# Attention and mixture-of-experts kernel: 64 value columns as the stationary operand of the attention product, w_v2 applied afterwards

## The reference

```python
xn = layernorm(x)
q, k = xn @ w_q, xn @ w_k                       # 64 columns each
p = softmax(where(causal, q @ k.T / 8, -inf))   # in each batch, 1024 x 1024
attention = p @ ((xn @ w_v1) @ w_v2)            # w_v1 128 x 64, w_v2 64 x 128
logits = xn @ w_router.T                        # 16
s = sigmoid(logits of the best expert e)
y = ((s * xn) @ up[e] * silu((s * xn) @ gate[e])) @ down[e]
shared = (silu(xn @ w_gate.T) * (xn @ w_up.T)) @ w_down.T
out = x + attention + shared + y
```

## Time and profile before

| what | before |
|---|---|
| time of the launch, three runs | 218.82, 219.39, 219.52 us; median 219.39 |
| span of the profiled execution | 222.3 us, which is its own time too (nothing lies around it) |
| PE, DVE, ACT, POOL busy | 207.7, 149.8, 128.7, 146.9 us |

### The profile page before, as it was taken

How to read it: one execution, slowest core, us unless ns; L and a number is a source line. 1 busy time by engine, 2 the same in 40 slices (tenths; PEclk the granted TensorE clock), 3 DMA queues, 4 the chain that set the end, 5 groups by cost and what they waited for, 6 DMA issues and landing times.

```text
span 222.3 us, 4940 instructions
## 1 busy us (share of the span) xinstructions
PE 207.7 (93%) x1405; PEld 180.4 (81%) x1405; DVE 149.8 (67%) x358; ACT 128.7 (58%) x305; POOL 146.9 (66%) x278
## 2 busy tenths in 40 slices
PE   4999999999999999999997999999999989967993
PEld 4787888887777898899895878999997969845893
DVE  2986969879767578868783648766664666425733
ACT  2475977876566756867756356444444436536641
POOL 3465785930388888888831378898989898872200
PEclk9999999999999999999999999999999999999999
DMA  5999999994063118215423222223232321004963
GB/s 156 291 383 306 222 265 175 156 238 201 13 173 103 36 39 200 74 44 141 127 56 79 51 67 73 80 60 90 78 92 63 86 75 41 3 0 156 312 195 97
DMA packets 26951, 28.30 MB, mean 127 GB/s; under 512 B 2579, under 2 KB 23066, under 8 KB 26288
## 3 DMA queue, kind: packets, MB, share of 16 engines
q1 hardware_dynamic: 24400, 23.77, 42.5%
q0 software_dynamic: 2528, 4.24, 6.1%
HBM read 14.28 MB, written 10.50 MB: 111 GB/s over the span
## 4 chain that ended last, share of the span: by engine, by line
PE 66%; issue 11%; POOL 11%; DVE 3%; DMA 3%; ACT 3%; another core or an unknown queue 1%; POOLq 0%; SPq 0%; ACTq 0%; DVEq 0%
PE acc L1368 13%; PE mid L1349 7%; PE acc L1235 6%; PE big L1175 5%; POOL y_rows L515 5%; PE big L1177 4%; PE big L1176 4%; PE acc L1454 4%; PE big L1336 4%; PE big L1333 4%; DMA xe<-scratch 3%; PE big L1368 2%; PE mid L1185 2%; PE mid L1205 2%; PE acc L1196 2%
## 5 line engine op out<-in xcount | busy, mean ns | idle before, releaser
L515 POOL DMA_INDIRECT y_rows<-y,ids x47 | 46.9, 998 | 11.9 <-issue 8.3
L463 POOL DMA_INDIRECT scratch<-rows,slot x32 | 34.2, 1067 | 17.8 <-DVE slot L744 12.7
L1368 PE MATMUL acc<-vr_all,pt 128*128 128x128 f32 x246 | 35.7, 280 | 4.0 <-issue 2.3
L1368 PEld LDWEIGHTS acc<-vr_all,pt 128*128 128x128 f32 x246 | 31.6, 191 | 6.2 <-issue 4.4
L794 DVE TENSOR_REDUCE negmax<-big 128x1 f32<-128x128 f32 (+7 forms) x32 | 23.9, 755 | 14.4 <-PE big L1336 9.5
L1067 ACT COPY pt<-mid 128x512 f32<-128x512 f32 (+3 forms) x48 | 22.8, 476 | 17.8 <-PE mid L1349 14.4
L896 DVE COPY eht<-mid 128x512 f32<-128x512 f32 (+1 forms) x24 | 16.3, 681 | 24.5 <-PE mid L1443 16.4
L1140 ACT COPY y<-acc 128x256 f32<-128x256 f32 (+1 forms) x24 | 8.8, 367 | 36.7 <-PE acc L1454 23.6
L1055 ACT ACTIVATE prob<-big,negmax 128x128 f32<-128x128 f32 (+7 forms) x32 | 23.8, 743 | 10.7 <-DVE negmax L794 7.8
L1454 PEld LDWEIGHTS acc<-wed,eht 128*128 128x128 f32 x188 | 24.3, 191 | 3.3 <-issue 1.7
L1454 PE MATMUL acc<-wed,eht 128*128 x188 | 25.4, 277 | 0.5 <-DVE eht L896 0.4
(11 more groups left out here) (142 smaller groups left out, 465.0 us busy)
## 6 DMA issues: line engine op xcount, KB each, us to landing
we_raw<-w_gate_up SPq DMA_DIRECT2D x4, 1024.0 KB, 10.5
scratch<-blank SPq DMA_DIRECT2D x1, 3120.0 KB, 30.3
xe<-scratch SPq DMA_DIRECT2D x24, 130.0 KB
q_raw<-qk_all SPq DMA_DIRECT2D x8, 256.0 KB
k_raw<-qk_all SPq DMA_DIRECT2D x8, 256.0 KB
wed<-w_down SPq DMA_DIRECT2D x1, 2048.0 KB, 34.4
expert_out<-y_rows SPq DMA_DIRECT2D x8, 256.0 KB, 4.8
out<-res SPq DMA_DIRECT2D x7, 256.0 KB, 3.3
```

The source lines that it names most:

```text
L463: pool.indirect_dma_start(scratch, bass.IndirectOffsetOnAxis(ap=slot[:, t:t + 1], axis=0), rows[:, t, :], None).then_inc(row_sent[t % FLY] ...
L515: pool.indirect_dma_start(y_rows, bass.IndirectOffsetOnAxis(ap=ids[:, t:t + 1], axis=0), y[p % NY][:, t % 2, :], None, bounds_check=NT * P ...
L1368: last = pe.matmul(weighed(b, g, r), pt[n % 2][:, cols], v, start=kb == 0 and (r == 0 or own_bank), stop=True, skip_group_check=True)
```

## The change

- The product of w_v1 and w_v2 at the start goes (two more warm-up transposes stand in its place). `vr_all` holds 64 values and 16 logits for a tile: `project_logits` is 128x80 for each tile, and ACT takes four tiles in one copy. w_v2 gets a tile of its own, `wv2`, and a DMA of its own.
- `weigh(b, n)` is one FP32 product for a block. The 64 value columns of the key tile are stationary, the block in `pt` (up to 512 columns) moves. An even key tile writes to partitions 0 to 63 of `acc`, an odd one to 64 to 127, so in one or the other half of the array's columns.
- The sums of a half are then copied to `mixed` (`keep_mixed`: ACT for g = 0, DVE for g = 1), and `outputs(b, g)` multiplies them by w_v2, which stands there twice, once for the even and once for the odd sums: four 128x128 products for a half. For the last half of batch 3 these are `keep_last` and `last_output`, after all products of the batch. `add_attention` waits for these products (`mixed_out`, `last_out`) in place of those of `weigh`.
- There are four buffers `pt` instead of two, and PE runs the products in groups of four (or two, on the edges of the expert stage); transposes, scores and `outputs` move around them.

```diff
-    VR = P + NE
+    VR = KD + NE
...
-                           + [(f"pt{n}", [P, GC], F32) for n in range(2)])
...
+                           + [(f"pt{n}", [P, GC], F32) for n in range(PTS)]
+                           + [(f"mixed{g}", [P, GC], F32) for g in range(BG)])
...
+            sp.dma_start(wv2[:, :], w_small[:, V20:V20 + P]).then_inc(wv2_loaded, 16)
...
+            def keep_mixed(b, g):
+
+                dve.wait_ge(pv_done, FIRST + b * STEPS + (STEPS if g else GT))
+                dve.tensor_copy(mixed[g][:, :], acc[g][:, :]).then_inc(mixed_kept[g], 1)
...
-                    dve.wait_ge(pv_done, FIRST + b * STEPS + (STEPS if g else GT))
+                    dve.wait_ge(mixed_out[g], b + 1)
...
-                        dve.wait_ge(pv_done, FIRST + b * STEPS + 2 * GT + t + 1)
+                        dve.wait_ge(last_out, t + 1)
...
+                if not first:
+                    keep_mixed(b - 1, 1)
                 if b == B - 1:
+                    row_max(b, BT - 1)
                     add_attention(b - 1, 1)
-                    row_max(b, BT - 1)
                     return
...
-                act.copy(vr_all[:, g * GT:g * GT + GT - 1, :],
-                         mid[0][:, 0:(GT - 1) * VR].rearrange("p (t n) -> p t n", n=VR)).then_inc(vr_kept[u], 1)
-                act.copy(flat(vr_all[:, g * GT + GT - 1:(g + 1) * GT, :]), acc[u][:, 0:VR]).then_inc(vr_kept[u], 1)
+                act.copy(flat(vr_all[:, g * GT:(g + 1) * GT, :]), mid[0][:, 0:GT * VR]).then_inc(vr_kept[u], 1)
...
-                act.copy(pt[n % 2][:, c0:GC], mid[n % 2][:, c0:GC]).then_inc(pt_ready, 1)
+                act.wait_ge(pv_done, FIRST + b * STEPS + n + 1 - PTS if b or n >= PTS else FIRST)
+                act.copy(pt[n % PTS][:, c0:GC], mid[n % 2][:, c0:GC]).then_inc(pt_ready, 1)
...
+            def keep_last(part):
+
+                act.wait_ge(pv_done, FIRST + B * STEPS)
+                cols = slice(part * GC // 2, (part + 1) * GC // 2)
+                act.copy(mixed[1][:, cols], acc[1][:, cols]).then_inc(last_kept, 1)
...
                     keep_pt(b, 0)
+                    keep_pt(b, 1)
                     exp(b, BT - 2)
-                    keep_pt(b, 1)
                     keep_pt(b, 2)
+                    keep_pt(b, 3)
                     exp(b, BT - 1)
-                    keep_pt(b, 3)
+                keep_mixed(b, 0)
                 keep_pt(b, GT)
...
-            pe.matmul(mid[1][:, 0:P], ws_raw[0:KD, V10:V10 + P], ws_raw[0:KD, V20:V20 + P], start=True, stop=True
-                      ).then_inc(v12_done, 1)
...
-                for r in range(c0 // P, GT):
-                    cols = slice(r * P, (r + 1) * P)
-                    own_bank = isinstance(b, int) and b == B - 1 and g == 1
-                    last = pe.matmul(weighed(b, g, r), pt[n % 2][:, cols], v, start=kb == 0 and (r == 0 or own_bank),
-                                     stop=True, skip_group_check=True)
-                last.then_inc(pv_done, 1)
+                half = kb % 2 * KD
+                pe.matmul(acc[g][half:half + KD, c0:GC], flat(vr_all[:, b * BT + kb:b * BT + kb + 1, 0:KD]),
+                          pt[n % PTS][:, c0:GC], start=kb < 2, stop=True, skip_group_check=True
+                          ).then_inc(pv_done, 1)
+
+            def to_output(b, g, r):
+
+                keys = KD if g == 0 and r == 0 else P
+                return pe.matmul(weighed(b, g, r), mixed[g][0:keys, r * P:(r + 1) * P], wv2[0:keys, :], start=True,
+                                 stop=True, skip_group_check=True)
+
+            def outputs(b, g):
+
+                if b == 0 and g == 0:
+                    pe.wait_ge(wv2_loaded, 16)
+                pe.wait_ge(mixed_kept[g], b + 1)
+                for r in range(GT):
+                    last = to_output(b, g, r)
+                last.then_inc(mixed_out[g], 1)
+
+            def last_output(r):
+
+                pe.wait_ge(last_kept, r // 2 + 1)
+                to_output(B - 1, 1, r).then_inc(last_out, 1)
...
+                    transposes(b, 0)
+                    transposes(b, 1)
+                    if b < B - 1:
+                        scores(b, BT - 1)
+                    else:
+                        outputs(b - 1, 1)
+                transposes(b, 2)
+                transposes(b, 3)
+                for n in range(GT):
+                    weigh(b, n)
+                if not first and b < B - 1:
+                    outputs(b - 1, 1)
...
+                transposes(b, GT)
+                transposes(b, GT + 1)
+                outputs(b, 0)
+                transposes(b, GT + 2)
+                transposes(b, GT + 3)
...
+                scores(following, 0)
+                for n in range(GT, 2 * GT):
                     weigh(b, n)
...
+                for n in range(2 * GT, STEPS):
+                    weigh(b, n)
+                scores(following, GT + 1)
+                scores(following, GT + 2)
```

More of the change, by code:

```diff
@@ L1378, in first_half @@
                     pe.wait_ge(ranks_used, 1)
-                if b == B - 1:
                     transposes(b, 0)
-                    for n in range(GT):
-                        transposes(b, n + 1)
+                    scores(b, GT + 2)
+                    transposes(b, 1)
+                    scores(b, BT - 1)
+                else:
+                    transposes(b, 0)
+                    transposes(b, 1)
+                    if b < B - 1:
+                        scores(b, BT - 1)
+                    else:
+                        outputs(b - 1, 1)
@@ new lines, in first_half, with second_half @@
+                transposes(b, 2)
[4 more added lines that the diff above has]
+                    outputs(b - 1, 1)
+            def second_half(b, following):
+                if b == B - 2 and following is not None:
+                    scores(following, GT)
+                    transposes(b, LATER + 2)
+                    scores(following, GT + 1)
+                    transposes(b, LATER + 3)
+                    transposes(b, LATER + 4)
+                    scores(following, GT + 2)
+                    for n in range(LATER + 1, STEPS):
@@ L1383, in first_half @@
                         weigh(b, n)
+                    scores(following, BT - 1)
                     return
[L1385 to L1403 removed]
+                transposes(b, GT)
@@ new lines, in second_half @@
+                scores(following, 0)
+                for n in range(GT, 2 * GT):
+                    weigh(b, n)
+                scores(following, 1)
+                scores(following, 2)
+                transposes(b, 2 * GT)
+                transposes(b, 2 * GT + 1)
+                scores(following, 3)
+                scores(following, GT)
+                transposes(b, 2 * GT + 2)
+                transposes(b, 2 * GT + 3)
+                for n in range(2 * GT, STEPS):
+                    weigh(b, n)
```

151 lines of the change are left out of this document (74 added, 77 removed).

## The result

The changed kernel took 223.34 us (median of 5 runs, 222.11 to 223.58), the kernel before 219.2 (218.82 to 219.52): the ratio is 1.018, with a 95% interval of 1.016 to 1.021. It is 1.8% slower; I had forecast 222.6. The profiled execution of the changed kernel has a span of 220.4 us, less than the 222.3 of before.

What follows compares the result with a forecast made beforehand. PE was taken to bound the attention stage, POOL's scatters the expert stage. Expert start -0.9 - 1.7 + 3.3 + 1.6 = +2.3, last stage +0.9: 219.4 + 3.2 = 222.6 us, range 216.8 to 227.0.

Steps and rivals of the forecast that it cites:

- `step_experts` behind the adds, +1.6: Start of the expert stage on DVE: `add_attention(1, 1)` waits for `outputs(1, 1)`, so `step_experts` comes 1.6 us later.
- First stage, -0.9: Kernel start: shorter 80-column passes save 0.7 us and the dropped ACT copies 0.2; ends 0 and -1.4.
- Overlap, 4.9 for 8.0: Attention products on PE: both array halves work at once, so a batch's products take 4.9 us instead of 8.0.
- Products with w_v2, 1.8: Attention stage on PE: eight new products per batch, 16 passes, cost 1.8 us a batch.
- Change of form, 0.16: PE, between 128-column work and the new products: each change costs 0.16 us, six a batch; ends 0 and 0.25.
- Waits, +3.3: PE up to the end of `scores(2, 7)`: new waits (a) to (d) add 3.3 us together, range 0.8 to 4.
- (d): Part of the waits: transposes of the last blocks wait for copies queued behind exps, 0.5 us in all.
- (c): Part of the waits: `scores(1, 0)` waits for DVE's rounding of q, with no add in front, 0.5 us.
- Up to `scores(2, 7)`: Kernel start to the end of those scores: first stage -0.9, products and changes of form -1.7, waits +3.3.
- The clock: Rival, chance 0.10: after PE's wait of 3.6 us for expert rows, slow work costs 2.1 us, giving 224.7.
- Last stage, +0.9: End of the kernel: -0.8 up to `scores(3, 7)`, then +1.7 to DVE's last add; range -1.5 to +2.5.
- the rival "faster": Rival, chance 0.30: changes of form cost nothing and the last stage loses its waits, giving 217.5 us.

Runs made afterwards that it cites:

- e1: The changed kernel with `name_experts` moved ahead of `add_attention(1, 1)` on DVE: 223.29 us, 0.995 of the kernel before beside it.
- e5: The changed kernel with three moves on DVE (`name_experts`, `split_k` of batch 2 and the adding of the last returned rows, all earlier): 218.82 us, 0.997 of before.
- e7: The changed kernel with two groups of four products in batches 0 and 1 split in pairs, scores between them: 222.29 us, 1.013 of before.
- e4: The changed kernel, unchanged, measured and profiled again: 223.29 us, 1.018 of the kernel before.
- e6: The kernel before with `name_experts` moved ahead of `add_attention(1, 1)` on DVE: 220.17 us, 1.004 of the kernel before.
- the quiet set: The runs e4 to e7 and those of the kernel before beside them, which took 219.2 us; the other sets are called disturbed.
- e0: The kernel before, unchanged, run for a second profile: span 223.3 us; the kernel before took 225.2 us in that set.

## Why the prediction was right, point by point

- **Place and sign.** The loss lies where I put it: `step_experts`, and with it rows, scatters and keys. Forecast +2.3 for the start of the expert stage, measured +3.0 at the first scatter. e1 shows the cause, since moving `name_experts` alone brings the stage back, and e5 shows it in the time.
- **`step_experts` behind the adds, +1.6.** From the maximum of `scores(2, 7)` to the end of `name_experts` were 4.95 (109.00 to 113.95) and are 6.49 (110.68 to 117.17): +1.54.
- **First stage, -0.9.** This term was too large: the first scores start at 63.46 in place of 63.83, -0.4. The shorter product is a shorter pass in most groups: eight passes of 80 columns advance 0.81, 0.101 each, where eight of 144 columns advanced 0.89 (13.32 to 14.21 before).

```profile
13.26 1.01 PE L1236 MATMUL mid<-ws_raw,xt 128*128 128x80 f32 x8
14.07 0.47 PE L1208 MATMUL mid<-xth,wsh 128*128 128x512 f32 x1
```

But up to the last groups the gain is lost again in waits for other engines (0.39 for DVE at 19.69, 0.37 for POOL at 27.94): the groups at 24.11, 31.28 and 38.19 start only 0.04 earlier than before (24.15, 31.32, 38.23). That is the case that I had named as the end at 0; only the last groups keep their gain.

- **Overlap, 4.9 for 8.0.** 4.8 was measured a batch (1.44 + 1.87 + 1.51), its changes of form included. The pattern was too pessimistic: in it the second product starts only with the second pass of the first, and the rows of e7 show both first passes starting together. A pair takes 8 pass lengths plus the changes, not 12. The Trainium skill, "TensorE: Matmul & The Clock Gate", Part 3, gives a speedup of 2.38 for three column tiles; here four products of 512 columns gave 3.57 / 1.87 = 1.91 for two.
- **Products with w_v2, 1.8.** This was too small: 1.00 and 1.19, 2.2 a batch.
- **Change of form, 0.16.** Too large: 0.06 each. The Trainium skill, "TensorEngine Tiling (Array Packing)", Key Properties, says that a change of mode drains the engine; here e7's 0.12 is all that two changes can have cost.
- **Waits, +3.3.** Measured 0.95 at batch 0 (I had 1.1) and 0.77 at `scores(2, 0)` (1.2); the listed ones of 0.3 to 0.4 for copies and exps, four in batches 0 and 1, make 1.4 more, so 3.1 of idle. But idle is counted from the modelled end of the row before, and the start behind a wait comes later than it would have by more than that. Worked out from the starts, at 0.1117 for a pass, the six waits cost 1.4, 0.9 and four times 0.5, together 4.3. So the term was 1.0 too small, and its part (d), the copies and exps, was 0.5 in the sum and 2.0 in the trace; (c) didn't come. My clause that these waits eat the saved passes was right; that it was the groups of four that made part of them I had not seen, and e7 shows it.
- **Up to `scores(2, 7)`** I had +0.7, measured +1.7 (109.00 to 110.68). The first stage and the products with w_v2 add 1.2 and the waits 1.0; the groups of products with their changes, 4.8 a batch for 4.9 + 6 x 0.16, take 2.1 back. That makes 0.8, so 0.9 was in no term: some 0.45 a batch, in part in starts that come 0.05 to 0.1 late (eight transposes at 94.09 advance 0.96, not 0.89).
- **The clock.** This was a rival with a chance of 0.10, at 2.1 us; it came in most runs, at 1.2. Its condition was near, a wait of 3.6 (it was 2.9), and its chance far too low: idle of 1 us elsewhere is no evidence on one of 3. The Trainium skill, "TensorE: Matmul & The Clock Gate", Why this matters for your kernels, warns of idle gaps between bursts of matmuls for this reason; e4 agrees, at 1.16 us, and e5, with 0.76 of idle there, has no such stretch; but the first profile of the changed kernel, with a wait of 2.91, has none either, so the wait makes the fall likely and not certain.
- **Last stage, +0.9.** From the last keys to DVE's end: 20.8 in e6, which has the old products (194.21 to 215.03), 21.45 in the changed kernel, +0.65; the tail of 2.8 was 2.9. But to the end of the span it is 24.6 in e6 and 24.4 in the changed kernel (24.3 in e4): there the stores end the span, and the term is worth -0.2. That is one step that failed: I counted DVE's end as the kernel's. The other is that the 10.3 us from the keys to `scores(3, 7)` (194.00 to 204.34), of which PE idled 3.4, were those of a disturbed run: e6, with the old products, takes 6.0 (194.21 to 200.17) and idles 0.4. So most of the waits that the -0.8 and the rival "faster" were to win aren't the kernel's.
- **The sum.** +3.0 at the first scatter, +1.2 for the clock, -0.2 in the last stage: +4.0, for 4.1 measured. I had 2.3 + 0.9 = 3.2. The start of the experts was under-sized by 0.7, the clock wasn't in the sum, and a last stage counted 1.1 too high covered more than half of that. So the mechanism of the loss was right, but that 222.6 lies within 0.8 of 223.34 is in part luck.
- **POOL's pace.** It was right that the stream doesn't catch up: in the quiet set every profile has 72.2 us from the first to the last expert scatter, whatever came before it. That is 3.14 for a pair, e6 with its old products included; the 3.18 of the earlier trace rows held the 1.1 that the disturbed run lost.

## What to carry to other kernels

When a change makes an instruction wait, look at what stands behind it on its engine: here four adds of 1.1 us carried the one table on which 70 us of work start, and three moves on that engine turned 1.8% slower into 0.3% faster. Two half-width FP32 products overlap almost fully on the two halves of the array (1.87 us for 3.57), so a pair is enough to gain; splitting two groups of four in pairs here made results come some 0.2 us earlier a batch, and 0.7 where a pair also filled a wait. A wait of TensorE ahead of a dense stage can cost more than its length: here 1.2 us more than the 2.9 of the wait.

## What the runs showed of the hardware that I had not expected

- Two FP32 products of 64 stationary and 512 moving columns, each of two passes, take 1.01 us on different halves and about 1.8 on one half (3.65 for four). On different halves the first passes of both start together, at 78.99 in e7, and the second ones at 79.47.
- PE's results can come microseconds behind its rows with the granted clock at 1.00. DVE starts the maximum of scores 0.40 us behind the start of their last row in e6 (197.26 to 197.66), but 3.3 behind it in e0 (197.31 to 200.64) and 3.9 in the first profile of before (195.03 to 198.92). Such delays, and the stretch at the half clock that follows one in e0, lie in the 5 us that the last stage of these two profiles is longer; that they are most of the 6 us between the kernel before in one set (219.2) and another (225.2) is an inference. What causes them was not found.
- Past the first 20 us, the 14 profiles have eight waits of PE between 1.81 and 2.91 us. At seven of them the granted clock falls to 0.50 for a stretch, which begins between 0.5 us ahead of the wait's end and 1.5 us behind it; at the eighth, of 2.91 in the first profile of the changed kernel, it stays at 1.00. At PE's other waits, none over 1.36, no profile has such a stretch before PE's work ends.
